# A two-layer graph network on one core: ones set only where they are read, the first edge pass's side products begun 12 steps later, and its last 49 masks made by GpSimd

## The reference, cut to what matters

```
x = layernorm(x + L0(x))         # L0: segment_sum(weight * x[src], dst), then W1, W2, leaky relu, row norm
h = relu(tconv1(x)); x = layernorm(x + tconv2(h))
# tconv, 4 heads of 64:
q, k, v, e = x@Wq+bq, x@Wk+bk, x@Wv+bv, edge_attr@We
logits = sum_c(q[dst] * (k[src] + e)) / 8         # per head
a = softmax of logits over the edges with one dst
out = segment_sum((v[src] + e) * a, dst) + x@Ws + bs
```

## Time and profile before

| | us |
|---|---|
| median of 3 runs | 4563.72 (4563.23 to 4576.3) |
| profiled execution, own time | 4573.59 |
| its span | 4571.8 |
| first edge pass, in the span | 61 to 1053 |
| first attention pass, begin | 1304 |
| second attention pass, begin | 2974 |

### The profile page before, as it was taken

One profiled execution on the slowest core, in us unless ns is written; L12 is line 12 of the kernel. 1 busy time (PEld: TensorE's weight loads), 2 busy tenths in 40 slices (PEclk: granted clock), 3 DMA queues, 4 the chain that ended last, 5 costly groups with the idle time before them and its releaser, 6 DMA issues. The chain is left out here.

```text
span 4571.8 us, 108781 instructions
## 1 busy us (share of the span) xinstructions
PE 4165.2 (91%) x17818; PEld 3191.7 (70%) x17818; DVE 3800.5 (83%) x20658; ACT 2981.0 (65%) x10684; POOL 3159.2 (69%) x2982
## 2 busy tenths in 40 slices
PE   4999999998878999999999998979999999999988
PEld 3887777774546777777777775557777777777755
DVE  5555555557869999999999998879999999999986
ACT  2333333332317889898898896129999999999970
POOL 7677777760058778788787882188888888888840
PEclk9999999999989999999999999989999999999999
DMA  5887887774568888888888884578888888888844
GB/s 163 248 254 240 242 239 240 239 217 137 163 186 262 256 250 262 253 258 257 253 262 257 260 260 126 182 224 258 258 253 259 258 259 258 259 254 258 254 143 153
DMA packets 770799, 1064.69 MB, mean 233 GB/s; under 512 B 111308, under 2 KB 588586, under 8 KB 770135
## 3 DMA queue, kind: packets, MB, share of 16 engines
q0 software_dynamic: 171184, 540.40, 39.6%
q1 hardware_dynamic: 598952, 517.34, 37.4%
HBM read 906.14 MB, written 151.16 MB: 231 GB/s over the span
## 5 line engine op out<-in xcount | busy, mean ns | idle before, releaser
L1446 POOL DMA_INDIRECT e_kv<-kv,src x1664 | 1661.7, 999 | 503.9 <-issue 295.9
L1680 ACT ACTIVATE e_vals<-e_kvj,e_ex 128x65 f32<-128x65 f32 x6572 | 1687.0, 334 | 0.2
L1468 PE MATMUL e_q<-q,e_pick 128*128 x3328 | 1058.8, 400 | 152.3 <-DVE e_logit L1575 103.1
L1575 DVE CUSTOM_DVE_ANT_0 e_kvj<-e_kvj,e_q 128x64 f32<-128x64 f32 x6656 | 1063.5, 215 | 6.6 <-PE e_q L1468 3.1
L153 POOL DMA_INDIRECT rows_x<-x_rows,rows_src x783 | 745.3, 952 | 252.6 <-issue 171.0
L1468 PEld LDWEIGHTS e_q<-q,e_pick 128*128 128x128 f32 x3328 | 580.4, 191 | 441.9 <-issue 377.3
L1563 DVE TENSOR_TENSOR e_kvj<-e_kv,e_e 128x512 f32<-128x512 f32 x1110 | 753.4, 679 | 67.6 <-DMA e_kv<-kv,src 52.0
L1510 PE MATMUL e_sum<-e_vals,e_mask 128*128 128x260 f32 x2536 | 785.2, 391 | 21.2 <-ACT e_vals L1680 10.8
L1458 PE MATMUL e_e<-e_we,e_ea 112*128 112x256 f32 x2220 | 672.3, 384 | 38.5 <-DMA e_ea<-attr_tiles 38.4
L1437 POOL TENSOR_SCALAR e_pick<-e_spots,own 128x512 f32<-128x512 bf16 x416 | 692.4, 1664 | 15.5 <-DMA e_spots<-locals 1.9
L1636 DVE TENSOR_TENSOR acc<-acc,e_sum 128x260 f32 x1602 | 669.1, 418 | 36.7 <-PE e_sum L1510 26.5
(11 more groups left out here) (226 smaller groups left out, 4883.2 us busy)
## 6 DMA issues: line engine op xcount, KB each, us to landing
e_ea<-attr_tiles SPq DMA_DIRECT2D x1110, 112.0 KB
edges<-q SPq DMA_DIRECT2D x277, 256.0 KB
e_made<-edges SPq DMA_DIRECT2D x554, 128.0 KB
e_spots<-locals SPq DMA_DIRECT2D x416, 128.0 KB
q<-attr_tiles SPq DMA_DIRECT2D x277, 112.0 KB
e_kv<-kv,src POOLq DMA_INDIRECT x1664
e_plain<-masks SPq DMA_DIRECT2D x396, 64.0 KB
masks<-q SPq DMA_DIRECT2D x208, 64.0 KB
```

Source lines behind the costliest of these rows:

```text
L1446: e.indirect_dma_start(out=kv[:, u, :], out_offset=None, **rows_of(kv_rows, k["src"][:, i:i + 1])).then_inc(kv_got[u], 16)
L1468: e.matmul(pe_q[i % 2][:, 0:D], pick[:, c, at:at + P], rows, start=True, stop=True).then_inc(q_done, 1)
L1575: dot = e.tensor_tensor_reduce(kvj[:, i % 2, h, 0:C], kvj[:, i % 2, h, 0:C], pe_q[i % 2][:, hs], 1.0, 0.0, ALU.mult, ALU.add, logit[:, j % ...
L1680: by_weight = e.activation(vals[:, n % R, h * HV:(h + 1) * HV], kvj[:, 2 + n % NV, h, :], ACT.Copy, scale=ex[:, b % 2, h, r:r + 1])
```

## The change: what it does

It has three parts. In the first edge pass the edge products are spread over steps 12 to 774, where it was steps 0 to 774; their number is unchanged. In the same pass the masks of steps 783 to 831 are made by GpSimd behind its last gather, with a semaphore of their own (`late_masked`), where VectorE made them. In the attention passes only the 65th column of each head of the 44 value slots is set to 1.0, by VectorE, as the seventh of its small sets; GpSimd sets nothing, and `ones_set` is gone.

```
-    edges_due = due(s.trios, BUSY)
+    BUSY, FIRST, LATE = T - s.blocks - 8, 12, s.tiles
+    edges_due = {FIRST + i: c for i, c in due(s.trios, BUSY - FIRST).items()}
...
 gpsimd, first pass
             for i in range(begun, s.tiles):
                 ring.gather(e, i)
+            for i in range(LATE, T):
+                e.wait_ge(summed, i - R + 1)
+                e.tensor_scalar(mask[:, i % R, :], k["iota"][:], k["local"][:, i:i + 1], ring.weight[:, i:i + 1],
+                                ALU.is_equal, ALU.mult).then_inc(late_masked, 1)
 tensor, first pass
-                e.wait_ge(masked, i + 1)
+                e.wait_ge(masked, min(i + 1, LATE))
+                if i >= LATE:
+                    e.wait_ge(late_masked, i - LATE + 1)
 vector, first pass
-                if i < T:
+                if i < LATE:
...
 gpsimd, attention
-                e.memset(kvj[:], 1.0).then_inc(ones_set, 1)
-                e.wait_ge(ones_set, 1)
 vector, attention
-                e.wait_ge(cleared, 6)
-                e.wait_ge(ones_set, 1)
+                e.memset(kvj[:, 2:, :, C:HV], 1.0).then_inc(cleared, 1)
+                e.wait_ge(cleared, 7)
 sync, attention, load_runs(0)
-                        e.wait_ge(cleared, 6)
+                        e.wait_ge(cleared, 7)
```

More of the change, by code:

```diff
@@ L599, in edge_pass_weighted @@
     T, R, SUMS = s.steps, 6, 4
-    BUSY = T - s.blocks - 8
+    BUSY, FIRST, LATE = T - s.blocks - 8, 12, s.tiles
     mask = ph.sb("mask", [P, R, P])
@@ L604, in edge_pass_weighted @@
     edges = EdgeProducts(ph, k, s, t, edge_table)
-    edges_due = due(s.trios, BUSY)
+    edges_due = {FIRST + i: c for i, c in due(s.trios, BUSY - FIRST).items()}
     plain = PlainMasks(ph, k, s, mask_table, k["q"][:, edges.width:])
     sums = [ph.psum(f"sum{u}") for u in range(SUMS)]
-    masked, added = ph.sem("masked"), ph.sem("added")
+    masked, late_masked, added = ph.sem("masked"), ph.sem("late_masked"), ph.sem("added")
     acc, summed = k["acc"], ring.summed
@@ L1298, in edge_pass_attention @@
         made_got, plain_got = ph.sems("made_got", 2), ph.sems("plain_got", 2)
-        w_got, cleared, ones_set = ph.sem("w_got"), ph.sem("cleared"), ph.sem("ones_set")
+        w_got, cleared = ph.sem("w_got"), ph.sem("cleared")
         e_done, q_done, kvj_done, dots_done, picked, apart_done = (
```

## The result

| | before | after |
|---|---|---|
| median time | 4571.77 us (8 runs, 4563.23 to 4578.81) | 4551.89 us (8 runs, 4548.84 to 4558.65) |
| span of the profiled execution | 4571.8 us | 4547.8 us |

The ratio is 0.9959, with a 95% interval of 0.9948 to 0.9970: 18.7 us less, 13.7 to 23.8. The forecast was 28.3 us less, 4535.4 us. So the kernel became faster, but a third of the forecast gain is missing. The two times, 4535.4 and 4551.9, lie 16.5 us apart, further than the two gains. 8.0 us of that belong to the starting point: the forecast counted from the median of three runs, 4563.7, and over eight runs the kernel before takes 4571.8. The measured time still falls inside the range of 4530 to 4552, by 0.1 us. That is luck and confirms nothing: it rests on where two unrelated errors, some 8 us of starting point and some 10 us of gain, happened to end.

A forecast was written before the change was run, and what follows sets the result against it. GpSimd's gathers were taken to bound the first edge pass, chained adds its end, GpSimd then VectorE the attention passes. Gains 9.1 + 0.8 + 9.2 + 9.2 = 28.3 us from 4563.7 gave 4535.4 us; 8-in-10 range 4530 to 4552.

The forecast's parts named there:

- Edge products from step 12, 9.1 us: First edge pass: gather 76's wait shrinks from 9.40 to 0.30 us, moving all 706 gathers behind it; gain 9.1 us.
- Rival C: First edge pass: step 49 comes only at 121 to 125 us; the products' gain is 4, time 4540; chance 0.07.
- none of the runs' spread lies in a place of the change: The runs spread over 13 us, and none of that was said to lie where the change touches the kernel.
- 49 masks on GpSimd, +0.8 us: End of first edge pass: at 0.6 us a mask, adds go from 0.637 to 0.62 us apart; gain 0.8 us.
- Rival A: End of first edge pass: masks take 0.84 us, costing 10.8 us; gain 17.5, time 4546; chance 0.20.
- behind it on GpSimd stands nothing until the node pass: End of first edge pass: no GpSimd work follows the late masks, so no cost was counted there.
- forecast's own signs of being wrong: Gap over 1 us ahead of gather 76, adds spaced by GpSimd's masks, or an attention pass shorter by under 8 us.
- Ones, 9.2 us in each attention pass: Start of each attention pass: without GpSimd's set of 10.06 us its gathers begin earlier; gain 9.2 us each.
- the 8 to 10 that should have shown it: Attention passes: expected sign that VectorE's first dot comes 8 to 10 us earlier.
- lower bound of 8.0: Attention start, from VectorE's side: first edge product ends near 1310.6, query follows at once instead of at 1318.58; gain 8.0.
- Rival B: Attention passes: VectorE's own work sets the end, so the 18.4 us go; gain 9.9, time 4554; chance 0.07.

The follow-up runs named there:

- after, again: The kernel after, unchanged, run once more beside the kernel with all masks on VectorE on one chip: 4550.8 us, ratio to before 0.9960.
- masks on VectorE: The kernel after with the last 49 masks of the first edge pass made by VectorE again: 4549.3 us, ratio to before 0.9942.
- the same, again: The kernel after with all masks on VectorE, run once more on the same chip as the kernel after: 4540.4 us, ratio to before 0.9944.
- products alone: The kernel before with only the edge products begun at step 12; masks on VectorE, ones set by GpSimd: ratio to before 0.9975.
- late masks alone: The kernel before with only the last 49 masks of the first edge pass moved to GpSimd: ratio to before 1.0022.
- ones alone: The kernel before with only the change to the ones of the attention passes: ratio to before 0.9972.
- DRAIN, then masks: The kernel after with an added GpSimd DRAIN behind its last gather and 35 late masks instead of 49: 4547.8 us, ratio to before 0.9954.
- masks on VectorE, bias later: The kernel after with all masks on VectorE and the skip path's bias made later in the first attention pass: 4544.4 us, ratio to before 0.9942.

## Why the prediction was right in direction and wrong in size

All stages, by the first instruction of VectorE (last node pass: of TensorE) in each trace:

| kernel | node pass | attention 1 | node pass 2 | attention 2 | last node pass | span |
|---|---|---|---|---|---|---|
| before | 1054.46 | 1304.52 | 2819.24 | 2973.72 | 4442.49 | 4571.8 |
| after | 1054.82 | 1307.02 | 2813.45 | 2967.52 | 4426.90 | 4547.8 |
| after, again | 1055.10 | 1307.29 | 2814.74 | 2967.79 | 4426.94 | 4565.9 |
| masks on VectorE | 1045.01 | 1296.95 | 2802.60 | 2957.03 | 4422.94 | 4554.3 |
| the same, again | 1045.12 | 1297.07 | 2800.04 | 2954.30 | 4416.26 | 4536.4 |
| products alone | 1047.18 | 1297.32 | 2813.03 | 2967.01 | 4437.07 | 4575.9 |
| late masks alone | 1064.00 | 1316.09 | 2834.56 | 2988.82 | 4464.95 | 4591.8 |
| ones alone | 1052.66 | 1304.61 | 2811.32 | 2965.45 | 4429.20 | 4558.3 |
| DRAIN, then masks | 1045.58 | 1297.74 | 2805.64 | 2960.43 | 4418.91 | 4546.4 |
| masks on VectorE, bias later | 1043.98 | 1295.93 | 2793.07 | 2946.94 | 4410.42 | 4543.3 |

- **Edge products from step 12, 9.1 us: right.** Gather 76 has the usual 0.30 ahead of it, the last gather is 8.9 us earlier. Over all ten traces of the table the last gather lies on average 8.6 us earlier with the part than without. Alone it gives 11 us (6 to 16), and where VectorE makes all masks, the pass is 5.5 to 10.5 us shorter, by which traces are paired. The pace behind step 0 was even better than assumed, 8.70 us for 13 sums, 0.67 instead of 0.85 each. Rival C is out. But the forecast's word that none of the runs' spread lies in a place of the change didn't hold: in the trace with the ones alone, which leaves this pass as it was, gather 76 waits 8.43 us, not 9.40.
- **49 masks on GpSimd, +0.8 us: wrong, and this is where the forecast failed.** Two things in it. First the price: 0.791 us instead of the 0.6 that I took between 0.40 and 1.585. The nearest row, the pick, gives 0.40 for a quarter of its columns, and the mask took twice that, not one and a half times. It has a second arithmetic step, but it also reads f32 where the pick reads bf16, and no run separates the two. Rival A was near, with 0.84 us, but its price of 49 x 0.22 us ignored the lead. Only the last 31 additions are spaced by the masks. They span 23.20 us, with all masks on VectorE 19.17, so 4.0 us more; and they start 0.6 us earlier, probably what came of the forecast 0.8, since VectorE has no masks to make beside them. Together the pace cost 3.45 us. Second, what was not in the sum at all: "behind it on GpSimd stands nothing until the node pass". What stands there is the DRAIN, 7.9 us from the last instruction, which makes the wait ahead of the node pass 6.35 us longer. It was in the trace of before, 7.8 us behind the last gather, hidden by 31 us of additions. Together -9.8 us instead of +0.8; 28.3 - 0.8 - 9.8 = 17.7 us is what the corrected sum gives, against 18.7 measured. One of the forecast's own signs of being wrong had come true with it, additions spaced by GpSimd's masks. Rival A's time of 4546 lies near the result, but by a mechanism of which it names only a third.
- By the Trainium skill (GPSIMD Engine Reference, section 4.1, Engine selection) elementwise work stays on VectorE, at about half the speed on GpSimd for two inputs and near line rate for one. The mask reads one full tile beside two columns, which is nearer the page's case of one input, and it came out at 0.791 / 0.342 = 2.3 times VectorE's. So the page's advice held and its word on one input did not, and the forecast set the advice aside for want of a row.
- **Ones, 9.2 us in each attention pass: right.** The first attention pass is 1514.7, 1515.7 and 1518.5 us long with the set on GpSimd, and 1503.0 to 1507.9 without (six traces, that with the bias moved left out), 10.1 us less on average. The second is 1468.8, 1470.1 and 1476.1 long against 1458.5 to 1465.9, 10.2 us less. The way there was right for GpSimd and wrong for the others. VectorE's first dot came 4.9 us earlier in the first pass of the kernel after and 6.8 in the second, not the 8 to 10 that should have shown it: TensorE's first edge product came 2.4 us later than before, and in the first pass VectorE waited for the bias. So the lower bound of 8.0, which took both for granted, had no footing. And yet the first pass was 8.3 us shorter in that pair of traces, since GpSimd's own stream bounds the next 120 us, as forecast. Its 19th pick mask, at 1439.00 before, 134.5 us behind VectorE's first instruction, stands at 125.7 now:

```profile
1432.68 1.59 POOL L1444 TENSOR_SCALAR e_pick<-e_spots,own 128x512 f32<-128x512 bf16 x1
```

  In the time alone the part gives 13 us (7 to 18), so its 18.4 lie at the edge. Rival B is out.
- **Not from the change:** the last node pass took 120.9 us in the profile after and 129.3 in that before, and in others 120.1 to 139.0, in the second profile of the kernel after the 139.0. It follows TensorE's granted clock: over that pass the column reads 0.96 and 0.98 where it took 120.9 and 120.1 us, 0.90 where it took 129.3, and 0.81 and 0.82 where it took 138.8 and 139.0. Windows of before, then of after, in its middle:

```profile
4500.00:4520.00 20.00, 18.54 (x65) 10.91 (x64) 14.07 (x64) 1.92 (x8) 0.00 (x0) 0.93 0.56 173
4520.00:4540.00 20.00, 20.00 (x57) 12.23 (x57) 12.20 (x56) 1.82 (x8) 0.00 (x0) 0.73 0.38 118
```

```profile
4500.00:4520.00 20.00, 19.91 (x75) 12.03 (x74) 15.50 (x71) 2.07 (x9) 0.00 (x0) 1.00 0.56 174
4520.00:4540.00 20.00, 18.18 (x67) 10.72 (x66) 15.69 (x71) 2.25 (x10) 0.00 (x0) 1.00 0.46 147
```

  The clock column reads 0.93 and 0.73 against 1.00. So the two spans, 24.0 us apart, overstate the change by this luck; at the begin of that pass they are 15.6 us apart. The first node pass took 250.1 us in the profile before and with the products alone, and 251.9 to 252.2 in all others of the table, the one with the ones alone included, which changes nothing ahead of it. The clock column there is 0.99 in before and 0.96 in after. Why it falls into one or the other is open, and with it 2 us.

The best version of those run is the change without its second part. Its ratio is 0.9942 and 0.9944 in two comparisons, about 26 us under the kernel before. Its node pass begins 9.8 and 10.0 us earlier than in the kernel after; by the time that second difference is 3 and 10 us in the two comparisons.

## What to carry to other kernels

Look at what closes a block before giving an idle engine work near its end: the DRAIN behind the engine's last instruction may be long, and so far hidden. Find its row in the trace, in that very block, and add what of its distance from the engine's last instruction nothing covers to the price. And moving work off an engine that has slack within a dependent chain (additions at 0.62 us) to one that makes it slower than the chain can only lose. Where the trace has no row of the same operation on the new engine, work out what the sum gives at the dearer end of what the nearest rows allow.

## What the hardware showed that I had not expected

- In the first edge pass GpSimd's first DRAIN behind its indirect gathers ends 7.8 to 7.9 us behind its last instruction, in all fourteen traces, and just as much when that instruction came 56 us after the last gather. In the attention passes it is 6.3 to 7.0 us, in the first two node passes, which have no gathers, the DRAIN ends 0.2 to 0.3 us behind. A second DRAIN with no gather between took 0.18 us, or ended within 0.1 us of its last mask.
- A mask with two arithmetic steps on 128 columns in f32 takes GpSimd 0.79 us (782 to 862 ns in the kernel after), VectorE 0.34.
- One chip ran the kernel before in 5087.6 us where others took 4570 to 4573. In the four kernels profiled on it the first edge pass ended at 1315 to 1318 instead of 1043 to 1056; single masks, additions and gathers took as long as elsewhere. In 300 to 1000 us its DMA moved 199 to 200 GB/s, on the others 240 to 242, and TensorE's granted clock was 0.93 to 0.95 against 0.98 to 0.99. Why is open. The ratio of a changed kernel there, 0.9948, was that of the other chips (0.9942).
